# First transfers and casts of a fused decoder block in smaller pieces, with the rest of the order moved a little

## What is computed

```python
x = _layernorm(x + _L0_attn_ref(x, Wq, Wk, Wv, Wo), axis=-1)      # 16 query heads in 4 groups, rope, softmax
x = _layernorm(x + _L0_xattn_ref(ctx, ctx, x, ssm_kernel, D, 8), axis=-1)   # long convolution of k*v, mixed by x
x = _layernorm(x + _L0_ffn_ref(x, W_gate, W_qkv), axis=-1)        # top-1 gate, shared k and v, causal attention
```

## Time and profile before

| | before |
|---|---|
| median of 3 runs | 323.4 us (322.43 to 323.41) |
| the profiled execution | 322.93 us, span of its instructions 321.1 us |
| PE busy | 305.8 us, 95% |
| DVE, ACT, POOL busy | 244.1, 231.1, 200.7 us |
| chain that ended last | PE 74%, DVE 13%, ACT 4%, issue 4%, DMA 2% |
| granted TensorE clock | 0.991 |

### The profile page before, as it was taken

The page is one execution under the profiler, slowest core; times in us unless marked ns, Lnnn a source line. Parts: engine busy times, 40 slices in busy tenths (PEclk is TensorE's granted clock), DMA queues, the critical chain, the costliest instruction groups (busy, mean ns, idle before and its releaser), DMA issues.

```text
span 321.1 us, 6269 instructions
## 1 busy us (share of the span) xinstructions
PE 305.8 (95%) x2073; PEld 241.7 (75%) x2073; DVE 244.1 (76%) x502; ACT 231.1 (72%) x693; POOL 200.7 (62%) x289
## 2 busy tenths in 40 slices
PE   6999899999999999999999999999999999999982
PEld 2788798889888888888888988877556666666650
DVE  2778968735876985775684998889989899987555
ACT  3699767868769867696686688634479777788890
POOL 0599766875573698477661278995987976721021
PEclk9999999999999999999999999999999999999996
DMA  6950212020010311404000000000000000000001
GB/s 188 328 238 1 65 36 98 3 90 9 0 35 2 98 34 36 163 2 142 0 2 1 2 1 1 2 0 3 0 3 0 18 1 3 16 3 26 9 18 49
DMA packets 5760, 13.87 MB, mean 43 GB/s; under 512 B 864, under 2 KB 3040, under 8 KB 5472
## 3 DMA queue, kind: packets, MB, share of 16 engines
q1 hardware_dynamic: 5456, 13.08, 12.3%
q10 hardware_dynamic: 272, 0.39, 0.4%
HBM read 12.42 MB, written 1.05 MB: 42 GB/s over the span
## 4 chain that ended last, share of the span: by engine, by line
PE 74%; DVE 13%; ACT 4%; issue 4%; DMA 2%; POOL 1%; POOLq 0%; DVEq 0%; ACTq 0%
PE bank L402 18%; PE bank L549 11%; PE bank L439 7%; PE bank L424 7%; PE bank L660 4%; PE bank L671 4%; PE bank L510 4%; PE bank L618 3%; DVE t_cos L1781 3%; PE bank L683 2%; PE bank L655 2%; DMA w_raw<-in_wqkv 2%; PE bank L533 2%; PE bank L528 2%; PE bank L530 2%
## 5 line engine op out<-in xcount | busy, mean ns | idle before, releaser
L2288 POOL TENSOR_TENSOR t_sin<-rot,sin 128x512 f32<-128x512 f32 x36 | 46.8, 1308 | 32.8 <-ACT rot L1129 29.4
L2316 POOL TENSOR_TENSOR prob<-prob,rden 128x512 f32<-128x512 f32 x32 | 35.2, 1104 | 38.0 <-DVE rden L1681 38.0
L1164 ACT ACTIVATE prob<-bank,neg_max 128x128 f32<-128x128 f32 x128 | 45.6, 375 | 10.8 <-DVE neg_max L1674 9.5
L1244 ACT ACTIVATE prob<-bank,fneg_max 128x128 f32<-128x128 f32 x128 | 36.7, 379 | 6.3 <-DVE fneg_max L1838 6.3
L549 PE MATMUL bank<-wo_hi,head_hi 128*128 128x256 f32 x128 | 40.3, 314 | 0.5 <-DVE head_lo L1723 0.4
L549 PE MATMUL bank<-wo_hi,head_lo 128*128 128x256 f32 x128 | 36.0, 281 | 0.0
L549 PE MATMUL bank<-wo_lo,head_hi 128*128 128x256 f32 x128 | 36.0, 281 | 0.0
L1128 ACT COPY rot<-bank 64x512 f32<-64x512 f32 x40 | 23.4, 585 | 15.6 <-PE bank L402 14.6
L402 PE MATMUL bank<-x_hi,w_hi 128*128 128x512 f32 x96 | 32.6, 421 | 1.7 <-DVE w_hi L1642 1.7
L1595 DVE TENSOR_TENSOR t_cos<-bank,cos 128x512 f32<-128x512 f32 x36 | 24.6, 686 | 12.0 <-ACT rot L1129 11.3
L2278 POOL TENSOR_TENSOR kv<-ctxT 128x256 f32<-128x256 f32 (+3 forms) x64 | 33.1, 550 | 0.2 <-PE bank L424 0.2
(11 more groups left out here) (132 smaller groups left out, 800.9 us busy)
## 6 DMA issues: line engine op xcount, KB each, us to landing
w_raw<-in_wqkv SPq DMA_DIRECT2D x4, 768.0 KB, 4.4
toep<-in_toep SPq DMA_DIRECT2D x8, 256.0 KB, 3.0
wo_raw<-in_wo SPq DMA_DIRECT2D x4, 512.0 KB, 4.6
x_raw<-in_xt SPq DMA_DIRECT2D x2, 512.0 KB, 5.4
ctxT<-in_ctx SPq DMA_DIRECT2D x1, 1024.0 KB, 4.7
x<-in_x SPq DMA_DIRECT2D x1, 1024.0 KB, 8.9
out<-x SPq DMA_DIRECT2D x8, 128.0 KB, 1.7
wf<-in_wf SPq DMA_DIRECT2D x1, 784.0 KB, 4.4
```

Source lines behind the costliest of these rows:

```text
L1164: last = act.activation(prob[:, k % 2, h * P:(h + 1) * P], score_bank[k % 2][:, h * P:(h + 1) * P], ACT.Exp, bias=neg_max[:, k % 2, h:h + ...
L1244: last = act.activation(prob[:, c % 2, h * P:(h + 1) * P], scored[:, h * P:(h + 1) * P], ACT.Exp, bias=fneg_max[:, c, h:h + 1])
L2288: pool.tensor_tensor(t_sin[:, par, :].rearrange("p (b t) -> p b t", b=BH), rot[:, par, :].rearrange("p (b t) -> p b t", b=BH), sin[:, :].u ...
L2316: pool.tensor_tensor(own, own, rden[:, k % 2, :].unsqueeze(2).to_broadcast([P, HG, P]), ALU.mult).then_inc(norm_done, 1)
```

## The change

Four things change at the front. x's first half comes in two transfers, one for each half `c` of the model dimension. The weights of K come alone on ACT's queue, those of Q0 and Q1 by a transfer of their own on SP's. The casts and subtractions follow these pieces, with semaphores of their own, and PE's first projection waits piece by piece. The lists of all engines are then in a slightly different order from there to the end; the steps themselves are the same.

```diff
@@ -343,24 +349,28 @@
             def load_w(n):
                 sp.wait_ge(w_lo_done, 2 * n)
+                if n == 1:
+                    sp.wait_ge(w_lo_first, 1)
                 sp.dma_start(w_raw[:, :, :], wqkv_d[:, W_LOADS[n], :, :]).then_inc(in_w, 16)
...
-            sp.dma_start(x_raw[:, :, :], xt_d[:, 0, :, :]).then_inc(in_xt, 16)
+            for c in range(C):
+                sp.dma_start(x_raw[:, c, :], xt_d[:, 0, c, :]).then_inc(in_x_first[c], 16)
+            sp.dma_start(w_raw[:, :, P:3 * P], wqkv_d[:, 0, :, P:3 * P]).then_inc(in_w_second, 16)
             sp.dma_start(w_raw[:, :, 3 * P:], wqkv_d[:, 0, :, 3 * P:]).then_inc(in_w, 16)
             sp.dma_start(cos[:, :], cos_d).then_inc(in_trig, 16)
             sp.dma_start(sin[:, :], sin_d).then_inc(in_trig, 16)
-            sp.wait_ge(in_xt, 16)
-            sp.wait_ge(in_w_first, 16)
+            sp.wait_ge(in_x_first[C - 1], 16)
+            sp.wait_ge(in_w_second, 16)
             sp.dma_start(ctxT[:, :, :, :], ctx_d).then_inc(in_ctx, 16)
...
-            sp.wait_ge(x_lo_done, 1)
+            sp.wait_ge(x_lo_first, C)
             sp.dma_start(x_raw[:, :, :], xt_d[:, 1, :, :]).then_inc(in_xt, 16)
@@ -389,16 +399,19 @@
                 for n, (wp, xp) in enumerate(((w_hi, x_hi), (w_hi, x_lo), (w_lo, x_hi))):
-                    if first and n == 1:
-                        pe.wait_ge(x_lo_done, 1)
-                    if first and n == 2:
-                        pe.wait_ge(w_lo_done, 1)
                     for c in range(C):
+                        if j == 0 and name == "K" and front:
+                            if n < 2:
+                                pe.wait_ge((x_hi_first, x_lo_first)[n], c + 1)
+                            elif c == 0:
+                                pe.wait_ge(w_lo_first, 1)
+                        if j == 0 and name == "Q0" and front and n == 2 and c == 0:
+                            pe.wait_ge(w_lo_done, 1)
@@ -451,13 +464,14 @@
             def front_project(name):
                 if name == "K":
-                    pe.wait_ge(x_hi_done, 1)
                     pe.wait_ge(w_hi_first, 1)
+                if name == "Q0":
+                    pe.wait_ge(w_hi_second, 1)
@@ -731,28 +745,28 @@
             front_scores(0, range(0, 3))
+            v_turn(0)
             front_scores(0, range(3, HG))
-            v_turn(0)
             front_scores(1, range(HG))
@@ -1097,7 +1111,7 @@
-            act.dma_start(w_raw[:, :, 0:3 * P], wqkv_d[:, 0, :, 0:3 * P]).then_inc(in_w_first, 16)
+            act.dma_start(w_raw[:, :, 0:P], wqkv_d[:, 0, :, 0:P]).then_inc(in_w_first, 16)
@@ -1114,8 +1128,16 @@
+            def split_x_first(c):
+                act.wait_ge(in_x_first[c], 16)
+                act.copy(x_hi[:, 0, c, :], x_raw[:, c, :]).then_inc(x_hi_first, 1)
+
+            def second_w_high():
+                act.wait_ge(in_w_second, 16)
+                act.copy(w_hi[:, :, P:3 * P], w_raw[:, :, P:3 * P]).then_inc(w_hi_second, 1)
@@ -1260,210 +1282,211 @@
-            split_x(0)
+            split_x_first(0)
+            split_x_first(1)
+            second_w_high()
             split_w(0, 1)
...
+            front_copy_vT()
             split_x(1)
-            front_copy_vT()
+            copy_v(0)
             split_wo(0)
-            copy_v(0)
             exps(0, 0)
@@ -1639,10 +1663,16 @@
-                dve.tensor_copy(w_hi[:, :, 0:3 * P], w_raw[:, :, 0:3 * P]).then_inc(w_hi_first, 1)
+                dve.tensor_copy(w_hi[:, :, 0:P], w_raw[:, :, 0:P]).then_inc(w_hi_first, 1)
+
+            def first_w_low():
+                split_lo(w_lo[:, :, 0:P], w_raw[:, :, 0:P], w_hi[:, :, 0:P], w_hi_first, 1, w_lo_first)
+
+            def split_x_first(c):
+                split_lo(x_lo[:, 0, c, :], x_raw[:, c, :], x_hi[:, 0, c, :], x_hi_first, c + 1, x_lo_first)
```

More of the change, by code:

```diff
@@ L200, in decoder_kernel @@
         wo_lo_done = sem("wo_lo_done")
+        in_x_first = [sem(f"in_x_first{c}") for c in range(C)]
         in_w_first = sem("in_w_first")
+        in_w_second = sem("in_w_second")
         in_w = sem("in_w")
@@ L459, in front_project @@
                     pe.wait_ge(w_lo_done, 2)
-                project(0, name, front_bank[name], first=(name == "K"))
+                project(0, name, front_bank[name], front=True)
             def front_scores(k, heads):
@@ L768, in _ @@
             values(1, 0)
+            turn(1, 1)
             item(1, "Q1")
-            turn(1, 1)
+            item(1, "Q2")
+            scores(1, 3)
+            item(1, "Q3")
             output(0, 3)
-            item(1, "Q2")
-            item(1, "Q3")
-            scores(1, 3)
             item(1, "C5")
@@ L866, in _ @@
             scores(5, 1)
-            item(4, "C23")
-            values(4, 2)
-            turn(4, 3)
             item(4, "C24")
-            output(4, 1)
             item(4, "C25")
             item(4, "V")
+            turn(4, 3)
+            values(4, 2)
+            output(4, 1)
+            scores(5, 2)
+            values(4, 3)
+            v_turn(5)
             item(5, "K")
-            v_turn(5)
-            values(4, 3)
             turn(5, 0)
             output(4, 2)
-            scores(5, 2)
             item(5, "Q0")
@@ L931, in _ @@
             v_turn(7)
+            turn(7, 0)
             scores(7, 3)
-            turn(7, 0)
             mix_turn(0)
@@ L1083, in _ @@
             fturn(6, 3)
+            y_turn(5)
             fscores(7, 1)
@@ L1902, in _ @@
             split_x(1)
+            value_low(0)
             row_max(0, 0)
-            value_low(0)
             row_max(0, 1)
@@ L1959, in _ @@
             add_item(1, "Q3")
             prob_low(1, 2)
+            invert(1, 3)
+            row_max(2, 0)
             head_low(1, 1)
+            value_low(2)
             cos_item(2, "K")
-            value_low(2)
-            row_max(2, 0)
             row_max(2, 1)
-            add_item(2, "K")
-            head_low(1, 2)
             prob_low(1, 3)
             invert(2, 0)
+            accumulate(0, 1)
+            head_low(1, 2)
+            add_item(2, "K")
+            row_max(2, 2)
@@ L2009, in _ @@
-            prob_low(3, 0)
+            cos_item(3, "K")
+            add_item(3, "K")
+            split_w(2, 1)
+            head_low(2, 3)
+            invert(3, 1)
+            prob_low(3, 0)
+            cos_item(3, "Q0")
+            cos_item(3, "Q1")
+            row_max(3, 2)
+            row_max(3, 3)
             add_item(3, "Q0")
@@ L2217, in _ @@
             frow_max(4, 3)
-            mix_norm(6)
+            ffn_apply(1)
             share(5)
@@ L2245, in _ @@
             share(7)
+            ffn_norm(3)
+            ffn_apply(3)
             frow_max(7, 0)
             frow_max(7, 1)
+            ffn_norm(4)
+            ffn_apply(4)
             y_invert(5)
-            ffn_apply(4)
+            y_scale(5)
+            ffn_norm(5)
             frow_max(7, 2)
-            y_scale(5)
             frow_max(7, 3)
             y_invert(6)
-            ffn_norm(5)
             y_scale(6)
```

604 lines of the change are left out of this document (298 added, 306 removed).

## The result

The changed kernel takes 321.44 us (median of 6 runs, 321.37 to 321.61), the kernel before 323.4 (6 runs). The ratio is 0.9944 with an interval of 0.9927 to 0.996: 1.8 us or 0.56% faster. The medians themselves are 1.96 apart; the runs of the kernel before spread from 322.43 to 324.07. The profiled execution took 321.38 (span 319.6), against 322.93 before, so the two traces are 1.55 us apart.

What follows compares the result with a forecast made beforehand. PE, busy 95% of the span, was taken as the bound, with a front chain of first data, K, ACT's turn and POOL. 1.9 + 0.5 - 0.5 = 1.9 us gained gave 321.2; own range 319.5 to 322.3, wider 319.4 to 323.2.

Steps and rivals of the forecast that it cites:

- first case: Whole kernel: the pieces gain at the front and the new order keeps it, 319.5 to 322.3 us; chance 0.62.
- The sum of 1.9: Whole kernel: 1.9 gained by 40 us, 0.5 gained in the middle, 0.5 lost at the end.
- middle, to the last masks: From 40 to 300 us: 0.5 us gained, bounds 2 gained and 1.5 lost; no work added or dropped.
- last stage: Kernel's end: DVE's dearer list between block 7's maxima delays the copy PE waits for; 0.5 us lost, between 0 and 0.9.
- The second half comes no later than 5.9: Front: x's second half lands at 5.4, at latest 5.9, where ACT's cast of the whole x had started.
- The term 1.9: Front, up to 40 us: 1.9 us gained, bounds 0.9 (ACT's lead alone) and 2.8 (all PE's front waits).
- 0.9 + 1.07 is more than PE's own 1.9: From 20 to 40 us: ACT's 0.9 lead plus the 1.07 us wo_hi cast leaving this stretch let PE keep 1.9.
- sign of error: From 20 to 40 us: the forecast called itself wrong if PE waits over 1 us there.
- lower bound of 0.9: Gain by 40 us: at least 0.9 us, if only ACT's lead is left.
- rival 4: Last stage: four holds of DVE by POOL cost 2.75 us instead of 0.5; 323.3, up to 324.3; chance 0.10.
- Rival 2: Front hands on only 0.9 us and the end takes 0.5 to 0.9, given back by the order; 322.7; chance 0.18.
- Rival 3: Front: the pieces land no sooner, K's weights at 6.7 as before, only casts are shorter; 322.1 us; chance 0.10.

## Why the prediction was right, and where its steps were not

The forecast of 321.2 against 321.44 and the range of its first case hold, and the front gains by the mechanism that it named. The sum of 1.9 met 1.55 in the profiled runs, and 1.8 by the ratio of all runs. That it is so near is in part luck, since its terms missed in both directions:

| term | predicted | measured |
|---|---|---|
| K's first matmul | 5.7 | 5.35 |
| x's second half lands | 5.4, no later than 5.9 | cast at 6.70 |
| ACT casts the last weights | 7.78 | 8.39 |
| Q0 starts | 8.0 (2.0 earlier) | 8.89 (1.07 earlier) |
| ACT turns K | 8.6 to 8.7 | 9.25 |
| head 3's scores | 17.05 | 17.58, `v_turn` at 17.05 |
| second half's K | 19.3 (1.9 earlier) | 19.80 (1.43 earlier) |
| lead where the lists are level again | 1.9 at 40 us | 1.06 at 45 us |
| middle, to the last masks | +0.5 | +0.73 at the mask of 302.48 |
| last stage | -0.5 | -0.24, with -0.47 at the copy |

*Front: mechanism right, size wrong.* The step that failed is "The second half comes no later than 5.9; with a third of the competing weights I take 5.4." The whole x's landing was taken as a bound on its second half. It is none, and the cut of x itself is what broke it: with K's weights just as much apart and x whole, x is cast at 5.41, and in two pieces the last of the second half's 16 landings comes at 6.67. K's first matmul missed in the other direction, which changed nothing: the six kernels with this front start it anywhere from 5.20 to 6.22 and Q0 at 8.71 to 8.98, because K's second matmul waits for x's second half. By 4 us ACT's queue had moved 0.06 MB before and 0.10 MB after. The transfers in the first 4 us after (queue: packets, MB, share; then issue, KB, us to landing):

```profile
q1 hardware_dynamic: 181, 0.34, 32.0%
q10 hardware_dynamic: 212, 0.10, 8.7%
...
w_raw<-in_wqkv ACTq DMA_DIRECT2D x1, 128.0 KB, 4.1
```

SP's queue, on which x stands first, fell from 0.43 MB to 0.34 in that time. The prediction also let ACT's last cast go at its old time because the bytes ahead of it are the same; it went 0.6 later. There too 15 of 16 landings were in by 7.68, before the old start of 7.78, and the last came at 8.37. The Trainium skill, "DMA: Bandwidth & Descriptors", section "Issuing engines are not separate DMA queues", says that transfers run on the same 16 engines and interleave, whichever engine starts them. The trace agrees as far as it goes: both queues moved bytes in the same 4 us, and SP's moved less when ACT's moved more. It doesn't say which piece ends last; that took the runs. The term 1.9 should have been 1.4. The part worked out without a transfer was right: `v_turn` lay in PE's wait, and the second half's K gained 0.53 more than ACT's turn had (0.44 predicted).

*First unit: the argument failed.* "0.9 + 1.07 is more than PE's own 1.9" counted the removal of the cast of wo's high part as helping PE. Putting it back in the changed kernel cost nothing: ACT had gaps of 1.2 to 1.6 there. And the wait that did come was in neither the sum nor a rival. The prediction's sign of error, PE waiting over 1 us between 20 and 40, came true with 1.67. The rows before could have warned: the addition at 26.78 took 1.31, against 0.68 where it stands alone, and ended 0.55 after POOL's pair of products. POOL's `wo_lo` lay at 28.95 to 31.34 then, behind the addition; the new list brings it forward to 27.29. The lead at 45 us, 1.06, lies near the lower bound of 0.9 that was given for ACT's lead alone. That is luck: ACT's lead is not what set it, but a front that gained 1.43 and this wait.

*Middle: right in size, and now placed.* The prediction said that what the new order adds can't be read from rows. It is 0.93 in the last attention unit, less the 0.28 of the new wait at 189.91. There a step that PE waits for (`head_lo`) was moved ahead of one that no wait of PE there hangs on; that this move by itself is worth the 0.60 is read from the rows, no run has it alone. Only kernels with the new lists have it.

*End: mechanism right, half the size.* The third maximum, 1.69 behind the last mask before and 2.80 now, is 1.1 late (1.3 predicted). The copy did end up behind the apply that waits for POOL's root, and 0.47 later against the mask of 302.48 than before (0.23 against the last mask). But the end itself lost only 0.24, half of the 0.5: the other 0.23 came back because PE's last matmuls ran at the higher clock, which was in no sum. The four holds of rival 4 are all there, 0.66, 0.66, 0.84 and 0.67, 2.83 in all against 2.75. The first lay in the room of the wait of 2.65 that DVE had before, the next two in that of 2.28. The last lay ahead of the copy with nothing to cover it. The fifth hold, 0.61 at 310.54, has the place of a wait of 1.35 for POOL that DVE had at 312.62 before. The kernel with the copy ahead shows what the placement was worth: 1.0 us, more than half of the whole change.

*The rivals.* Rival 2 describes the first unit in part: it took 0.37 of the front's 1.43 back, and the last unit returned more than that. Rival 3 is refuted for K's weights (landed 4.1 us after issue, their cast 1.9 sooner than before), and holds for x's second half. The rule that the prediction took from the Trainium skill, "DMA: Bandwidth & Descriptors", section "Rules for kernel authors", is one large transfer instead of several. It fits x, which gained nothing by the cut, and not the weights: those of K land 4.1 us after their issue as a transfer of their own, and 6.0 us after it as a part of the large one.

*What stays open.* The cut of x makes its second half late, by the last of 16 landings. Why that one lags isn't settled: with the cut there are more packets of fewer bytes and one more issue ahead of the rest, and no run separates them. With the halves on two queues both were in by 4.89, and K's weights came late instead. The wait left in the last stage (ACT's `t_sin` and the exponentials) wasn't worked on.

## What to carry to other kernels

A transfer cut in pieces brings its first piece sooner and may bring its last piece later than the whole did; the whole's landing is no bound. Ask which of all the pieces that the first step needs is the last, and cut only what moves that one. On an in-order queue, put the step that another engine waits for ahead of a step that itself waits for a third engine: one such swap in the last stage was worth 1.0 us. When the list of one helper engine is moved against another's, look for pairs of steps that slow each other before counting the move as free.

## What the runs showed of the hardware

DVE's addition of two tensors in SBUF took 0.68 us alone. It took 2.77, 2.76 and 2.32 beside POOL's 2.4 us subtraction, each time ending about 0.55 after POOL's instruction. DVE's product with one operand in PSUM kept its 0.69 (687 ns, the mean of all 36 in the changed kernel). That agrees with the Trainium skill, "SBUF — State Buffer", section "SBUF: two separate sides": DVE and GpSimd share a port pair that is locked for a whole instruction, taken by a DVE operation with two SBUF inputs against a GpSimd operation that reads SBUF, and the loser waits for all of it. What the trace adds is the price in a full schedule: one such meeting held DVE's queue for 2.1 us, and PE waited 1.67 behind it. With the meeting moved one place on, that wait was 0.5 and another of 0.6 came.
